# Cross attention to 257 keys: row maxima taken one head group at a time, with picks and one copy in another order

## The chip, the cores and the metric

One core of a Trainium2 chip. The metric is the device time of one execution of the whole kernel in microseconds (us); less is better. PE is TensorE's matmul, PEld its weight load, DVE VectorE, ACT ScalarE, POOL GpSimd, SP the engine that issues most DMAs.

## The reference

A four-layer perceiver-like model on x of shape (128, 32, 128), with a context of (128, 257, 128). Three of its sublayers are cross attention of 32 queries per batch to the 257 context rows, 16 heads of width 8, 128 batches each. The one with a mask (the other two are alike but for weights and biases):

```python
query = _split_heads(q @ wq.T + bq)
key_h = _split_heads(k @ wk.T + bk)
value = _split_heads(v @ wv.T + bv)
scores = jnp.einsum('bhqd,bhkd->bhqk', query, key_h) * scale
scores = jnp.where(mask == 0, jnp.float32(-1000000000.0), scores)
attn = jax.nn.softmax(scores, axis=-1)
x = jnp.einsum('bhqk,bhkd->bhqd', attn, value)
return x.transpose(0, 2, 1, 3).reshape(...) @ wo.T + bo
```

The result is added to x. The other sublayers (self attention, routed experts, a linear transformer, retention, feed-forward blocks) are not touched by the change.

## The kernel before

The function `cross_attention` runs three times, as a_cross, e_cross and t_cross; t_cross has the mask, and e_cross also collects the results of experts that ran before it (GpSimd fetches them, VectorE adds them). Each run is one block in which every engine has its own program, written out by hand as a function `step(i, n)`: i counts turns, n the N = 8 batches of a turn, and `turns` repeats it as a hardware loop over 128 batches. Order on an engine is the order of these calls; between engines only semaphores order the work.

Per batch the 16 heads form G = 4 groups of 4 heads. The scores of a group, 128 rows (4 heads x 32 queries) by 257 keys, fill one PSUM bank of their own, banks 0 to 3. The fifth bank (K_BANK) holds kT's projection of the next batch and, later in the step, the second turned half of E; the sixth (V_BANK) the projected values and, beside them, side products; the seventh (T_BANK) the first turned half; the eighth (O_BANK) the weighted values of four batches.

- TensorE, step n: scores(n) (line 2332; 2337 adds the mask), after all four exponentials of n - 1; the projection of the keys of n + 1 (line 2316), after ScalarE has copied the second half of n - 3 out of the same bank; side products; first turn of n - 2 (line 2390); values' projection of n + 1 (2320); second turn of n - 2 (2390), which waits for VectorE's copy of the projected keys, in the same bank; weighted values of n - 3 (2400).
- VectorE, step n: reciprocals of n - 1 (2530); in each fourth step (n % 4 = 3) three picks (2567), which add the right rows of O_BANK into aT, each after the one before; maxima of groups 0 and 1 in one instruction (2520); copy of the projected keys with their bias (2534); maxima of groups 2 and 3; the fourth pick; statistics in each fourth step; copy of the first turned half of n - 2 (2526); other side work (2548, 2542, 2555), which waits for ScalarE's values' copy of n + 1.
- ScalarE, step n: in each fourth step the copy that begins aT (2453); copy of the values of n (2471); copy of the second turned half of n - 3 (2467); side copies; four exponentials (2477), one per group, with the row sums. The first waits for the first pair of maxima, the third for the second pair; each reads its group's column of negtop.
- GpSimd, step n: E times the reciprocals for n - 1 (2251), and side work.

The maxima are double-buffered in negtop. The values and E have a buffer for each of eight batches.

Of the kernel before, what the change touches and what calls it, by code (L numbers as in the profile page):

```python
# [2113 lines left out]
def cross_attention(core, name, weights, context, scale, mask=None, rest=None, behind=None):  # L2114
# [10 lines left out]
    N, G, J = 8, 4, 4  # L2125
# [4 lines left out]
    with Scope(core, name) as sc:  # L2130
# [35 lines left out]
        s_score, s_top, s_exp, s_inv, s_unit = sc.sem("score"), sc.sem("top"), sc.sem("exp"), sc.sem("inv"), sc.sem("unit")  # L2166
# [16 lines left out]
        def exists(i, n):  # L2183

            return not isinstance(i, int) or 0 <= i * N + n < B

        def tile_exists(i, t):

            return not isinstance(i, int) or 0 <= i * 2 + t < TILES
# [5 lines left out]
        def turns(eng, step, written=1):  # L2195

            for i in range(written):
                for n in range(N):
                    step(i, n)
            with eng.Fori(written, TURNS - 1) as i:  # L2200
                for n in range(N):
                    step(i, n)
            for n in range(N + 7):
                step(TURNS - 1, n)
# [8 lines left out]
        @block.sync  # L2213
        def _(sp):
            fetch(sp)
            for h in range(2):
                sp.dma_start(ctx_sb[:, h], context[:, h]).then_inc(s_ctx[h], 16)
            if rest is not None:
                rest[0](sp)
            if mask is not None:  # L2220
                for j in range(4):
                    sp.dma_start(mask_int[j * S:(j + 1) * S], mask).then_inc(s_mask, 16)
            with sp.Fori(1, TURNS) as i:
                for h in range(2):
                    sp.wait_ge(s_vl, i * 2 - 1 + h)
                    sp.dma_start(ctx_sb[:, h:h + 1], context[:, bass.ds(i * 2 + h, 1)]).then_inc(s_ctx[h], 16)
# [202 lines left out]
        @block.scalar  # L2429
        def _(act):  # L2430
            arrived(act)
            act.wait_ge(s_ready, 1)

            def queries(i, t):
                act.wait_ge(s_qp, i * 2 + t + 1)
                act.activation(qT[:, t % 2], psum[:, V_BANK, SIDE], ACT.Identity, bias=bq[:], scale=scale).then_inc(s_q, 1)

            def turned(i, t):
                act.wait_ge(s_turned, i * 2 + t + 1)
                if tile_exists(i, t - 2):  # L2440
                    act.wait_ge(s_qp, i * 2 + t - 1)
                act.activation(hT[:, t % 2], psum[:, V_BANK, BESIDE], ACT.Copy).then_inc(s_hT, 1)

            def begin(i, n):

                t = n // 4
                if n % 4 == 2 and tile_exists(i, t - 1):
                    if exists(i, n + 1):
                        act.wait_ge(s_vp, i * N + n + 2)
                    act.wait_ge(s_alone, i * 2 + t)  # L2450
                    if tile_exists(i, t - 3):
                        act.wait_ge(s_out, i * 2 + t - 2)
                    act.activation(aT[:, (t - 1) % 2], psum[:, V_BANK, SIDE], ACT.Copy).then_inc(s_begun, 1)

            def side_out(i, n):

                t = n // 4
                if n % 4 == 0 and tile_exists(i, t + 1):
                    queries(i, t + 1)
                if n % 4 == 2 and tile_exists(i, t + 2):  # L2460
                    turned(i, t + 2)

            def second_half(i, n):
                act.wait_ge(s_t1, i * N + n + 1)
                if exists(i, n - 2):
                    act.wait_ge(s_pv, i * N + n - 1)
                act.activation(ET[:, n % 2, 1], psum[:, K_BANK], ACT.Copy).then_inc(s_ET1, 1)  # L2467

            def values_out(i, n):
                act.wait_ge(s_vp, i * N + n + 1)  # L2470
                act.activation(v_sb[:, n % N].rearrange("p c d -> p (c d)"), psum[:, V_BANK, 0:2 * P], ACT.Copy).then_inc(s_v, 1)

            def exponentials(i, n):
                for g in range(G):
                    if g % 2 == 0:
                        act.wait_ge(s_top, (i * N + n) * 2 + g // 2 + 1)
                    act.activation(E[:, n % N, g], psum[:, g, 0:SK], ACT.Exp, bias=negtop[:, n % 2, g:g + 1],  # L2477
                                   accum_out=total[:, n % 2, g:g + 1]).then_inc(s_exp, 1)

            def step(i, n):  # L2480
                begin(i, n - 1)
                if exists(i, n):
                    values_out(i, n)
                if exists(i, n - 3):
                    second_half(i, n - 3)
                side_out(i, n - 1)
                if exists(i, n):
                    exponentials(i, n)

            turned(0, 0)  # L2490
            queries(0, 0)
            turned(0, 1)
            turns(act, step)

        @block.vector
        def _(dve):
            def statistics(i, t):
                u, at = t % 2, i * 2 + t
                if tile_exists(i, t - 2):
                    gate(dve, s_centred, at - 1, passed)  # L2500
                dve.bn_stats(stats[:, u], x_tile(i, t)).then_inc(s_stats, 1)
                gate(dve, s_stats, at + 1, passed)
                dve.bn_aggr(moments[:, u], stats[:, u]).then_inc(s_moments, 1)
# [9 lines left out]
                dve.tensor_copy(fold_bf[:], spread(core.const("fold"), J, 1)).then_inc(s_mask_ready, 1)  # L2513
                dve.tensor_scalar(mask_neg[:], mask_int[:], 0.0, -1e30, ALU.is_equal, ALU.mult).then_inc(s_mask_ready, 1)

            def maximum(i, n, half):
                if half == 0:
                    dve.wait_ge(s_score, i * N + n + 1)
                at = slice(2 * half, 2 * half + 2)
                dve.tensor_reduce(negtop[:, n % 2, at], psum[:, at, 0:SK], AX.X, ALU.max, negate=True).then_inc(s_top, 1)  # L2520

            def first_half(i, n):
# [5 lines left out]
            def reciprocals(i, n):  # L2528
                dve.wait_ge(s_exp, (i * N + n) * G + G)
                dve.reciprocal(inverse[:, n % 4], total[:, n % 2]).then_inc(s_inv, 1)  # L2530

            def keys(i, n):
                dve.wait_ge(s_kp, i * N + n + 1)
                dve.tensor_scalar(kT[:, n % 2], psum[:, K_BANK, 0:SK], w("bk"), None, ALU.add).then_inc(s_k, 1)
# [23 lines left out]
            def pick(i, t, places):  # L2558

                out = aT[:, t % 2].rearrange("p (b s) -> p b s", s=S)  # L2560
                for j in places:
                    if j == 0:
                        dve.wait_ge(s_begun, i * 2 + t + 1)
                        dve.wait_ge(s_pv, i * N + 4 * t + 4)
                    else:
                        dve.wait_ge(s_picked, (i * 2 + t) * 3 + j)
                    dve.scalar_tensor_tensor(out=out, in0=psum[:, O_BANK].rearrange("p (b j s) -> p b j s", b=BPT, s=S)[:, :, j],
                                             scalar=in_group[:, j:j + 1], in1=out, op0=ALU.mult, op1=ALU.add
                                             ).then_inc(s_aT if j == J - 1 else s_picked, 1)
# [11 lines left out]
            def step(i, n):  # L2581
                picks = n % 4 == 3 and tile_exists(i, n // 4 - 1)
                if exists(i, n - 1):
                    reciprocals(i, n - 1)
                if picks:
                    pick(i, n // 4 - 1, (0, 1, 2))
                if exists(i, n):
                    maximum(i, n, 0)
                if exists(i, n + 1):
                    keys(i, n + 1)  # L2590
                if exists(i, n):
                    maximum(i, n, 1)
                if picks:
                    pick(i, n // 4 - 1, (3,))
                if rest is not None and isinstance(i, int) and i == 0 and n == 0:
                    rest[1](dve)
                if n % 4 == 0 and tile_exists(i, n // 4 + 2):
                    statistics(i, n // 4 + 2)
                if exists(i, n - 2):
                    first_half(i, n - 2)  # L2600
                ahead = (i, n - 3) if n >= 3 else (i - 1, n + N - 3)
                if fetch_of(*ahead) is not None:
                    add_result(fetch_of(*ahead))
                if n % 4 == 1 and tile_exists(i, n // 4 - 1):
                    last_weights(i, n // 4 - 1, n + 1)
                if n % 4 == 1 and tile_exists(i, n // 4 - 2):
                    output(i, n // 4 - 2, n + 1)
                if n % 4 == 3 and tile_exists(i, n // 4):
                    last_values(i, n // 4, n + 1)
# [914 lines left out]
```

## Time and profile before

| | |
|---|---|
| median of 3 runs | 3989.83 us (3988.98 to 3995.96) |
| the profiled execution | 3982.57 us |
| its span, first to last instruction | 3980.8 us |
| busy over the span: PE, DVE, ACT, POOL | 3385.2 (85%), 2670.8 (67%), 2362.3 (59%), 2422.3 (61%) us |
| mean granted TensorE clock | 0.925 of full speed |
| first and last scores' matmul of a_cross, e_cross, t_cross | 18.1 to 502.3, 2145.2 to 2630.0, 2887.7 to 3373.1 us |

The three stages lie at the start, in the middle and late in the span; together they are some 1455 of 3981 us. A share over the whole span says little of them. A step of n can be told in the timeline by its scores' matmul, and n % 4 by the side work: the picks stand in n % 4 = 3, the statistics in n % 4 = 0. I call the steps with n % 4 = 0, 1, 2, 3 A, B, C and D.

### The profile page before, as it was taken

The page shows a single profiled execution, that of the slowest core. Times are in us where ns is not written, and L with a number is a line of the kernel's source. Part 1 is how long each engine was busy: PE and PEld are TensorE (multiplying, and loading weights), DVE is VectorE, ACT ScalarE, POOL GpSimd, SP SyncE. Part 2 cuts the span into 40 slices and gives each one's busy share as a digit, 9 for nine tenths or more (in the row PEclk, how much of TensorE's full clock was granted, in tenths as well). Part 3 has the DMA queues.
Part 4 walks back from the last instruction along what each step waited for, and adds up shares of the span by engine and source line. Part 5 has one row for each costly group of instructions (what it writes and reads, how often), then busy time and mean ns, then how long its engine had stood idle before and what let it go on. Part 6 is the DMA issues. An engine that isn't in the chain of part 4 may idle for free. (4 is left out here: it accounts for less than half of the span.)

```text
span 3980.8 us, 119953 instructions
## 1 busy us (share of the span) xinstructions
PE 3385.2 (85%) x44674; PEld 2469.3 (62%) x44674; DVE 2670.8 (67%) x7002; ACT 2362.3 (59%) x6308; POOL 2422.3 (61%) x2724
## 2 busy tenths in 40 slices
PE   7999959999999579698698999978499999786866
PEld 5777737777777467365466777745277777453444
DVE  6888757777777523477445888857778887754655
ACT  6777736666666334386124777745577777644633
POOL 6767656776777343574425887746367676845733
PEclk9999979999999689898799999989599999887968
DMA  2111110000000122101221111110011111000023
GB/s 75 36 42 36 36 70 6 8 11 11 8 6 2 63 72 77 47 14 47 67 72 59 51 45 42 37 60 4 17 37 36 42 36 30 3 2 6 2 93 94
DMA packets 90549, 149.05 MB, mean 37 GB/s; under 512 B 10112, under 2 KB 66816, under 8 KB 89664
## 3 DMA queue, kind: packets, MB, share of 16 engines
q1 hardware_dynamic: 79936, 122.87, 9.9%
q0 software_dynamic: 10240, 20.99, 1.7%
q8 instruction: 261, 4.28, 0.4%
q14 instruction: 112, 0.92, 0.1%
HBM read 112.76 MB, written 31.06 MB: 36 GB/s over the span
## 5 line engine op out<-in xcount | busy, mean ns | idle before, releaser
L2251 POOL TENSOR_TENSOR t_cross_E<-t_cross_E,t_cross_inverse 128x1028 f32<-128x1028 f32 x128 | 243.2, 1900 | 134.8 <-DVE t_cross_inverse L2530 134.8
L2251 POOL TENSOR_TENSOR a_cross_E<-a_cross_E,a_cross_inverse 128x1028 f32<-128x1028 f32 x128 | 243.2, 1900 | 132.8 <-DVE a_cross_inverse L2530 132.8
L2477 ACT ACTIVATE t_cross_E<-t_cross_psum,t_cross_negtop 128x257 f32<-128x257 f32 x512 | 238.8, 472 | 113.5 <-DVE t_cross_negtop L2520 110.0
L2477 ACT ACTIVATE a_cross_E<-a_cross_psum,a_cross_negtop 128x257 f32<-128x257 f32 x512 | 238.8, 472 | 112.4 <-DVE a_cross_negtop L2520 103.9
L2477 ACT ACTIVATE e_cross_E<-e_cross_psum,e_cross_negtop 128x257 f32<-128x257 f32 x512 | 238.8, 472 | 111.2 <-DVE e_cross_negtop L2520 103.3
L2251 POOL TENSOR_TENSOR e_cross_E<-e_cross_E,e_cross_inverse 128x1028 f32<-128x1028 f32 x128 | 243.2, 1900 | 94.2 <-DVE e_cross_inverse L2530 94.1
L3090 PEld LDWEIGHTS l_psum<-l_ffn_w,l_hidden 128*128 128x128 f32 x1536 | 197.9, 192 | 98.0 <-issue 56.1
L3090 PE MATMUL l_psum<-l_ffn_w,l_hidden 128*128 128x128 f32 x1536 | 207.8, 278 | 19.0 <-POOL l_hidden L2963 17.9
L3083 PE MATMUL l_psum<-l_hT,l_ffn_w 128*128 128x512 f32 x384 | 200.6, 625 | 0.9 <-ACT l_hT L3139 0.9
L2520 DVE TENSOR_REDUCE t_cross_negtop<-t_cross_psum 128x2 f32<-128x514 f32 x256 | 175.8, 687 | 32.6 <-PE t_cross_psum L2337 31.7
L2520 DVE TENSOR_REDUCE a_cross_negtop<-a_cross_psum 128x2 f32<-128x514 f32 x256 | 175.4, 686 | 26.8 <-PE a_cross_psum L2332 26.4
L2520 DVE TENSOR_REDUCE e_cross_negtop<-e_cross_psum 128x2 f32<-128x514 f32 x256 | 175.6, 686 | 24.6 <-PE e_cross_psum L2332 24.5
L2942 POOL TENSOR_SCALAR l_normed<-inner,l_moments,l_rstd 128x128 f32<-128x128 f32 x192 | 149.8, 793 | 14.8 <-POOL l_rstd L2936 14.8
L2390 PE MATMUL e_cross_psum<-const_sb,e_cross_E 128*128 128x128 f32 x1024 | 154.3, 274 | 0.2
L2390 PE MATMUL a_cross_psum<-const_sb,a_cross_E 128*128 128x128 f32 x1024 | 153.4, 273 | 0.2
L2390 PE MATMUL t_cross_psum<-const_sb,t_cross_E 128*128 128x128 f32 x1024 | 153.4, 273 | 0.2
L2953 POOL TENSOR_TENSOR l_q<-l_q,l_q_stat 128x512 f32<-128x512 f32 x48 | 50.8, 1058 | 167.3 <-DVE l_q_stat L3217 167.3
L2963 POOL TENSOR_TENSOR l_hidden<-l_hidden,l_less 128x512 f32<-128x512 f32 x96 | 122.2, 1293 | 18.2 <-ACT l_hidden L3163 18.2
L1467 POOL DMA_INDIRECT slots<-hT_all,behind_place_i x64 | 61.7, 965 | 111.5 <-PE c_moe_psum L1600 61.9
L1467 POOL DMA_INDIRECT slots<-inner,a_moe_place_i x64 | 62.0, 969 | 101.6 <-PE a_moe_psum L1600 59.0
L3237 DVE TENSOR_TENSOR inner<-l_psum,inner 128x512 f32<-128x512 f32 x48 | 33.2, 692 | 132.1 <-PE l_psum L3075 132.1
L2390 PEld LDWEIGHTS e_cross_psum<-const_sb,e_cross_E 128*128 128x128 f32 x1024 | 121.2, 142 | 0.9 <-ACT e_cross_ET L2467 0.4
(754 smaller groups left out, 11124.1 us busy)
## 6 DMA issues: line engine op xcount, KB each, us to landing
a_cross_context<-context SPq DMA_DIRECT2D x32, 578.0 KB, 3.7
e_cross_context<-context SPq DMA_DIRECT2D x32, 578.0 KB, 3.7
t_cross_context<-context SPq DMA_DIRECT2D x32, 578.0 KB, 3.7
u_moe_weights<-pack_u_moe SPq DMA_DIRECT2D x1, 5633.0 KB, 16.3
slots<-l_blank SPq DMA_DIRECT2D x6, 832.0 KB, 12.2
a_moe_x_slots<-slots SPq DMA_DIRECT2D x26, 192.0 KB, 2.8
slots<-a_moe_y_slots SPq DMA_DIRECT2D x26, 192.0 KB, 2.1
c_moe_x_slots<-slots SPq DMA_DIRECT2D x26, 192.0 KB, 2.8
```

What stands on the lines that cost most here:

```text
L1467: pool.indirect_dma_start(slots.halves[g], bass.IndirectOffsetOnAxis(ap=place_i[:, k, at:at + 1], axis=0), rows[:, at], None).then_inc(s_p ...
L2251: pool.tensor_tensor(E[:, n % N], E[:, n % N], spread(inverse[:, n % 4], SK, 2), ALU.mult).then_inc(s_unit, 1)
L2390: last = pe.transpose(psum[:, (T_BANK, K_BANK)[c], g * P:(g + 1) * P], E[:, n % N, g, c * P:(c + 1) * P], ident)
L2477: act.activation(E[:, n % N, g], psum[:, g, 0:SK], ACT.Exp, bias=negtop[:, n % 2, g:g + 1], accum_out=total[:, n % 2, g:g + 1]).then_inc(s ...
L2520: dve.tensor_reduce(negtop[:, n % 2, at], psum[:, at, 0:SK], AX.X, ALU.max, negate=True).then_inc(s_top, 1)
L2942: last = pool.tensor_scalar(Y1[:, t], c.tile(t), moments[:, 0, t, 0:1], rstd[:, 0, 1, t:t + 1], ALU.subtract, ALU.mult)
L2953: pool.tensor_tensor(groups, groups, spread(q_stat[:, 2], DH, 2), ALU.mult).then_inc(s_soft, 1)
L2963: pool.tensor_tensor(hidden[:, f], hidden[:, f], less[:, f - 2], ALU.add).then_inc(s_late, 1)
L3083: pe.matmul(psum[:, U_BANKS[f % 2]], c.ffn(f * P), hT2[:], start=True, stop=True).then_inc(s_up, 1)
L3090: last = pe.matmul(psum[:, D_BANK, t * P:(t + 1) * P], hidden[:, f, t * P:(t + 1) * P], c.ffn((NF + f) * P), start=(f == 0 and t == 0), st ...
L3237: dve.tensor_tensor(c.chunk(), tiles(psum[:, C_BANK]), c.chunk(), ALU.add).then_inc(s_mid, 1)
```

## The change

The maxima are taken for one group at a time: four instructions of 128x257 in place of two of 128x514. Three of them now stand ahead of the keys' copy and one behind. The semaphore s_top counts four per batch, and each of ScalarE's exponentials waits for its own group's maximum. The picks of n % 4 = 3 were 0, 1, 2 ahead of the first maxima and 3 behind the last; now pick 0 is ahead of the maxima, pick 1 between the second and third maximum, picks 2 and 3 behind the fourth. On ScalarE the copy of the second turned half goes ahead of the values' copy where n is odd; where it is even the values stay first. Nothing else is changed; the arithmetic is the same.

```diff
@@ scalar: exponentials, step
                 for g in range(G):
-                    if g % 2 == 0:
-                        act.wait_ge(s_top, (i * N + n) * 2 + g // 2 + 1)
+                    act.wait_ge(s_top, (i * N + n) * G + g + 1)
                     act.activation(E[:, n % N, g], psum[:, g, 0:SK], ACT.Exp, bias=negtop[:, n % 2, g:g + 1],
...
                 begin(i, n - 1)
-                if exists(i, n):
+                if exists(i, n) and n % 2 == 0:
                     values_out(i, n)
                 if exists(i, n - 3):
                     second_half(i, n - 3)
+                if exists(i, n) and n % 2 == 1:
+                    values_out(i, n)
                 side_out(i, n - 1)
@@ vector: maximum, step
-            def maximum(i, n, half):
-                if half == 0:
+            def maximum(i, n, g):
+                if g == 0:
                     dve.wait_ge(s_score, i * N + n + 1)
-                at = slice(2 * half, 2 * half + 2)
+                at = slice(g, g + 1)
                 dve.tensor_reduce(negtop[:, n % 2, at], psum[:, at, 0:SK], AX.X, ALU.max, negate=True).then_inc(s_top, 1)
...
                 if picks:
-                    pick(i, n // 4 - 1, (0, 1, 2))
+                    pick(i, n // 4 - 1, (0,))
                 if exists(i, n):
                     maximum(i, n, 0)
+                    maximum(i, n, 1)
+                if picks:
+                    pick(i, n // 4 - 1, (1,))
+                if exists(i, n):
+                    maximum(i, n, 2)
                 if exists(i, n + 1):
                     keys(i, n + 1)
                 if exists(i, n):
-                    maximum(i, n, 1)
+                    maximum(i, n, 3)
                 if picks:
-                    pick(i, n // 4 - 1, (3,))
+                    pick(i, n // 4 - 1, (2, 3))
```

## Rows read from the trace of the kernel before

**Rows 1.** Windows view, first attention stage: us of window, busy per engine, clock, DMA.

```profile
16.00:506.00 490.00, 457.52 (x5145) 347.90 (x5145) 389.22 (x915) 375.70 (x1371) 339.03 (x342) 1.00 0.13 39
```

**Rows 2.** View of line 2520: who waited for it, us, times.

```profile
  ACT a_cross_E L2477: 103.9, 143
```

**Rows 3.** View of line 2332: ns min/median/max, first and last start.

```profile
L2332 PE MATMUL a_cross_psum<-a_cross_kT,a_cross_q_heads x1024: 375/450/792, 18.1 to 502.3; 32*128 32x257 f32 x171
...
L2332 PE MATMUL t_cross_psum<-t_cross_kT,t_cross_q_heads x1024: 375/450/792, 2887.7 to 3373.1; 32*128 32x257 f32 x171
```

**Rows 4.** Timeline, step A: start, length, engine, line, names, [idle before].

```profile
307.92 0.71 PE L2332 MATMUL a_cross_psum<-a_cross_kT,a_cross_q_heads 32*128 32x257 f32 x8
...
308.70 0.69 DVE L2520 TENSOR_REDUCE a_cross_negtop<-a_cross_psum 128x2 f32<-128x514 f32 x1 [0.15 <-PE a_cross_psum L2332]
...
308.77 0.67 PE L2316 MATMUL a_cross_psum<-a_cross_context,a_cross_weights 128*128 128x257 f32 x2
...
309.43 0.48 ACT L2477 ACTIVATE a_cross_E<-a_cross_psum,a_cross_negtop 128x257 f32<-128x257 f32 x1 [0.80 <-DVE a_cross_negtop L2520]
309.49 0.49 DVE L2534 TENSOR_SCALAR a_cross_kT<-a_cross_psum,a_cross_weights 128x257 f32<-128x257 f32 x1
...
309.89 0.68 DVE L2520 TENSOR_REDUCE a_cross_negtop<-a_cross_psum 128x2 f32<-128x514 f32 x1
...
310.39 0.60 PE L2390 MATMUL a_cross_psum<-const_sb,a_cross_E 128*128 128x128 f32 x4
...
310.61 0.48 ACT L2477 ACTIVATE a_cross_E<-a_cross_psum,a_cross_negtop 128x257 f32<-128x257 f32 x1
...
310.92 0.38 PEld L2400 LDWEIGHTS a_cross_psum<-a_cross_ET,a_cross_v 128*32 128x32 f32 x16 [0.17 <-issue]
...
311.07 0.47 ACT L2477 ACTIVATE a_cross_E<-a_cross_psum,a_cross_negtop 128x257 f32<-128x257 f32 x1
...
311.52 0.38 ACT L2471 ACTIVATE a_cross_v<-a_cross_psum 128x256 f32<-128x256 f32 x1
...
311.68 0.72 PE L2332 MATMUL a_cross_psum<-a_cross_kT,a_cross_q_heads 32*128 32x257 f32 x8
...
311.79 0.60 ACT L2467 ACTIVATE a_cross_ET<-a_cross_psum 128x512 f32<-128x512 f32 x1
```

**Rows 5.** Timeline, step D, the one ahead of it.

```profile
303.95 0.72 PE L2332 MATMUL a_cross_psum<-a_cross_kT,a_cross_q_heads 32*128 32x257 f32 x8
304.10 1.12 DVE L2567 SCALAR_TENSOR_TENSOR a_cross_aT<-a_cross_psum,const_sb,a_cross_aT 128x128 f32<-128x128 f32 x3
...
305.14 0.68 DVE L2520 TENSOR_REDUCE a_cross_negtop<-a_cross_psum 128x2 f32<-128x514 f32 x1
...
306.58 0.60 PE L2390 MATMUL a_cross_psum<-const_sb,a_cross_E 128*128 128x128 f32 x4
...
307.18 0.41 PEld L2400 LDWEIGHTS a_cross_psum<-a_cross_ET,a_cross_v 128*32 128x32 f32 x16 [0.24 <-issue]
```

**Rows 6.** Groups by form, VectorE maximum of 128 columns.

```profile
L1321 DVE TENSOR_REDUCE c_moe_best<-c_moe_cand 128x16 f32<-128x128 f32 x4 | 1.1, 286 | 0.1
```

**Rows 7.** Timeline, projection and second turn, steps C and B.

```profile
301.04 0.67 PE L2316 MATMUL a_cross_psum<-a_cross_context,a_cross_weights 128*128 128x257 f32 x2
...
302.76 0.60 PE L2390 MATMUL a_cross_psum<-const_sb,a_cross_E 128*128 128x128 f32 x4
...
312.54 0.67 PE L2316 MATMUL a_cross_psum<-a_cross_context,a_cross_weights 128*128 128x257 f32 x2
...
314.37 0.60 PE L2390 MATMUL a_cross_psum<-const_sb,a_cross_E 128*128 128x128 f32 x4
```

**Rows 8.** Timeline, stage with the mask: scores and first maxima.

```profile
3102.32 0.72 PE L2332 MATMUL t_cross_psum<-t_cross_kT,t_cross_q_heads 32*128 32x257 f32 x8
...
3103.18 0.69 DVE L2520 TENSOR_REDUCE t_cross_negtop<-t_cross_psum 128x2 f32<-128x514 f32 x1
```

**Rows 9.** Timeline, GpSimd, the stage that collects expert results.

```profile
2299.26 1.90 POOL L2251 TENSOR_TENSOR e_cross_E<-e_cross_E,e_cross_inverse 128x1028 f32<-128x1028 f32 x1 [1.41 <-DVE e_cross_inverse L2530]
```

## The prediction

> **What bounds the kernel now.** I first took the busy time of the engines over one of the three attention stages to 257 keys [rows 1]. No engine is full: TensorE shows 457.5 of 490 us, VectorE 389.2, ScalarE 375.7, GpSimd 339.0, at a granted clock of 1.00 (the 2.4 GHz level). Each engine waits for another one once per batch. The list of who waited for line 2520 then names the largest wait in the stage: ScalarE's exponentials wait 103.9 us for the negated maxima, in 143 places [rows 2]. The scores' matmuls show the length of a batch: from 18.1 to 502.3 us for 128 batches, less the 0.5 us that lie inside one batch, over 127 intervals, is 3.81 us; the stage with the mask takes the same (2887.7 to 3373.1) [rows 3]. Four batches, over which the side work repeats, take 15.24 us.
>
> Then the timeline of one step, n % 4 = 0, step A [rows 4]; times from here on are counted from the start of the scores' matmul, S (307.92). First pair of maxima +0.78, first exponential +1.51, kT projection +0.85, its copy by VectorE ("keys") +1.57, second pair +1.97, third exponential +2.69, fourth +3.15, next scores +3.76. The chain that sets the length: the copy of values and then of the second turned half (0.27 apart, 0.60 long) free the bank that kT's projection writes; the projection gives the keys' copy; behind that stands the second pair of maxima, and behind that the third exponential, which starts 0.04 after the pair ends (309.89 + 0.68 = 310.57, 310.61). Counted from e, the start of the fourth exponential: values +0.45, second half +0.72, its end +1.32, projection +1.46, keys' copy +0.72 later, second pair +0.40, third exponential +0.72, fourth +0.47: e to e is 3.77. That is steps A, B and C. In step D (n % 4 = 3) three picks of 1.12 us precede the first pair, which starts at +1.19 and not +0.78, and aT's copy delays the rest: 307.92 - 303.95 = 3.97 [rows 5]. Three times 3.77 and 3.97 are 15.28, against 15.24 measured, so I trust this chain.
>
> **The change part by part.** (1) *Four maxima of 257 in place of two of 514.* No row shows a 128x257 maximum. The pair of 514 takes 0.68 us [rows 4] and one of 128 columns 0.286 [rows 6]; the line between them gives 0.42 for 257. A VectorE instruction that waits for nothing starts 0.08 before the end of the one ahead (keys 309.49 with 0.49, then 309.89) [rows 4]. So a maximum takes 0.34 of the queue and a pair 0.68 - 0.08 = 0.60: the split costs 2 x (2 x 0.34 - 0.60) = 0.16 us of VectorE per batch. The gain: the first exponential waits for 0.42 and not 0.68, so it starts at +1.24 (+1.51 now). The bounds of the spacing are 0.34 and 0.42 (the full duration); I take 0.34, since the keys' copy has the same width and shows the overlap.
>
> (2) *Three maxima ahead of the keys' copy.* The third exponential no longer hangs on the projection. The maxima start at +0.78, 1.12, 1.46, the keys' copy at +1.80 to 2.28, the fourth maximum +2.20 to 2.62. Exponentials every 0.47: +1.24, 1.71, 2.18, 2.65; the fourth needs 2.62 + 0.04, so none waits again. Next scores by this route: 2.65 + 0.61 (311.07 to 311.68) = 3.26. The added waits of ScalarE for the second and fourth maximum are therefore met; queued behind them are only the exponentials and copies of the same step.
>
> But the keys' copy is now later after S, and the second turn on TensorE (it writes the bank that the copy reads) waits for it. Today the copy ends at +2.06 and that turn starts at +2.47, no stall. Afterwards it can start at +2.34 (2.28 + 0.06, the smallest wake-up in these steps, an estimate). From that turn to the end of the values' weight loads are 0.91 us (310.39 to 310.92 + 0.38) [rows 4], then the scores may load. In front of those loads stand the three waits of the scores; the weighted values, also behind waits long met, show 0.17 to 0.24 idle "issue" [rows 4, 5], so the gap is between 0 and 0.24 and I take 0.12. Route over TensorE: 2.34 + 0.91 + 0.12 = 3.37. This is what is late next, and step A becomes 3.37 us. The projection is not late for it: the scores now start later after e (3.73 - 2.91 = 0.82 at D to A), so it comes at 1.46 - 0.82 = +0.64.
>
> (3) *Second half ahead of the values in odd steps.* The bank is free at e + 1.05, so the projection comes 0.27 earlier. The values' copy comes at e + 0.93 and ends +1.31, before the side product that needs it; the next values' projection is later still. VectorE's three waits for a values' copy (last weights, output, last values) all name an even batch, whose order stays. In step B, whose turn comes 1.83 after the projection [rows 7], 0.55 + 1.83 = 2.38 against 2.34 from the keys: 3.41. Without this part the projection would be at +0.77 and the step 3.63: it is worth 0.2 us in two of four steps at most, since in D the keys decide anyway. Step C, with values first: projection 1.46 - 0.76 = +0.70, its turn 1.72 later [rows 7], 2.42: 3.45.
>
> (4) *Picks.* In D the first pick alone (about 0.35, after aT's copy) ends before the scores are there, so the first maximum is back at +0.78: a gain of 0.41. The second pick adds 0.26 to the queue (0.34 less the overlap) ahead of the keys: their copy ends at 2.54, the turn starts at 2.60, from there 1.01 (306.58 to 307.18 + 0.41) [rows 5] and 0.12: 3.73. The fourth exponential starts at 2.84 + 0.08 = about 2.91, next scores 3.52 by that route; TensorE decides. Picks three and four and the copy of the first half move behind the fourth maximum and end near +4.25, beyond the next scores by 0.5; the reader of that half comes 1.4 after those scores, and the next maximum waits for scores until +0.78: hidden, with about 0.1 to spare. If that cover is gone each 0.1 costs 32 x 0.1 = 3 us per stage.
>
> (5) *Sum.* 3.37 + 3.41 + 3.45 + 3.73 = 13.96 for four, 1.28 less, 32 times: 41 us per stage. With the mask the scores are ready 0.08 later (+0.86 for +0.78) [rows 8]; today the projection hides that, afterwards it is on the path in all four steps: 14.28, gain 31. In the stage that also collects expert results GpSimd idles 1.41 us per four batches in its first half [rows 9], so its floor is 15.24 - 1.41 = 13.83, just under 13.96; I take 39. Together 111 us. The profiled execution is 3982.57 us (span 3980.8), 7.3 below the median of 3989.83; 3982.6 - 111 = 3871.6, and on the median 3878.8.
>
> The page "VectorE: DVE Perf Modes" of the Trainium skill, section "The DRAIN you can't avoid", speaks against this change: it says that the next operation does not start until the pipe has emptied, and advises fewer operations. The trace does not show it so strictly (the 0.08 us overlap above); by the rule the spacing would be the full 0.42 us, which is the first rival below.
>
> **The rivals.** *Spacing equal to the duration* (0.42 between maxima, 0.34 behind a pick): keys end at 2.52, turn 2.58, step 3.61 three times; D has keys to 2.86, turn 2.92, step 4.05. Sum 14.88, gain 11.5 us in two stages and none with the mask: 3967 us. Against it: the keys' copy and the pair behind it overlap [rows 4].
>
> *TensorE's busy time is a floor.* 457.5 of 490 us [rows 1] leaves 32.5 per stage, 97.5 in all: 3892 us. Against it: busy times overlap; the second turn's 0.60 us end at 310.99, behind the next loads' start at 310.92 [rows 4]. The skill's page "Trainium Kernel Development and Optimization", section "Performance Expectations", calls matmul busy time a bad metric for this reason.
>
> *Slower: a single maximum costs nearly what a pair costs.* Place: VectorE's queue between the scores and the keys' copy, with the second turn behind it. Each us of spacing over 0.34 counts three times per step: 13.96 + 12 x (s - 0.34) = 15.24 gives s = 0.45 as the point from which the change loses. At the pair's 0.60 the four steps take 17.1, 1.85 more, 32 x 3 times: 4167 us. Against it: the 128-column maximum at 0.286 shows that width is paid for. For it: the margin is only 0.11 us, and the width of 257 was not measured.
>
> *It does nothing that counts*: an unseen wait (a context load, GpSimd) holds the step at 15.2: 3990 us. The waits of before show none.
>
> **How the numbers follow.** Forecast 0.72 (3836 to 3920); spacing 0.08; TensorE's floor 0.09; slower 0.06; nothing 0.05. The low end is the gap at zero in front of the scores (13.48 per four, 56 + 56 + 46 us gained: 3832), which I cut slightly; the high end goes halfway to the first rival (0.38 of spacing: 13.96 + 0.48, about 3925) and a little over, 3935. Left outside are the rivals at 3967, 3990 and 4167, 0.19. A difference of 0.2% (8 us) is about what can be told from none: faster 0.90, within 0.04, slower 0.06.
>
> **What would show it.** Right: 128x257 maxima of 0.42 us at 0.34 spacing; no wait of the exponentials for the maxima after the first; scores that start behind the values' loads and not behind the exponentials; VectorE's idle nearly gone; 13.9 to 14.0 us per four batches, a bit more with the mask. Wrong: maxima of over 0.5 us, a second turn later than +2.6 in steps A to C, a first maximum later than +0.8 in A (tail of D uncovered), GpSimd without idle time in the collecting stage, or a granted clock under 1.00 there.

## The result and the profile after

| | before | after |
|---|---|---|
| median | 3989.4 us (4 runs) | 3963.6 us (3962.2 to 3967.4, 4 runs) |
| ratio | | 0.993, 95% interval 0.9915 to 0.9945 |
| span of the profiled execution | 3980.8 us | 3960.4 us |
| four batches, a_cross, e_cross, t_cross | 15.23, 15.25, 15.27 us | 14.85, 14.83, 15.23 us |

The change brings 26 us where 111 were forecast; the time lies outside the range of the prediction, and the direction is right. The last row of the table is worked out as in the prediction, from the first and the last scores' matmul (less 0.5 us, over 127 intervals, times 4). Its savings of 0.38, 0.42 and 0.04 us, 32 times each, are 27 us, which is all of the difference; the stage with the mask gained next to nothing. The ratio is taken from the runs; the stages are read from one profiled execution of each kernel.

The view of the scores' line after the change, answering to [rows 3]: line, engine, count, length in ns (min/median/max), first and last start in us.

```profile
L2332 PE MATMUL a_cross_psum<-a_cross_kT,a_cross_q_heads x1024: 375/474/792, 18.1 to 490.2; 32*128 32x257 f32 x171
...
L2332 PE MATMUL e_cross_psum<-e_cross_kT,e_cross_q_heads x1024: 375/474/792, 2135.8 to 2607.2; 32*128 32x257 f32 x171
...
L2332 PE MATMUL t_cross_psum<-t_cross_kT,t_cross_q_heads x1024: 375/474/792, 2866.5 to 3350.5; 32*128 32x257 f32 x171
```

The maxima, now at line 2521, and who waited for them, answering to [rows 2]:

```profile
L2521 DVE TENSOR_REDUCE a_cross_negtop<-a_cross_psum x512: 411/415/427, 19.4 to 491.9; 128x1 f32<-128x257 f32 x171
...
  ACT a_cross_E L2476: 107.5, 158
```

The windows view of the first stage, answering to [rows 1]:

```profile
16.00:506.00 490.00, 461.59 (x5213) 353.01 (x5213) 401.50 (x1196) 369.53 (x1374) 344.44 (x347) 1.00 0.14 41
```

A single maximum takes 0.415 us, as interpolated, and the granted clock is 1.00 as before. But ScalarE waits for the maxima as long as before, 107.5 us against 103.9: the wait was not removed, it moved. Ahead of the first exponential of step A it is 1.25 us now and was 0.80 in [rows 4]. VectorE is 401.5 us busy of 490, not nearly full, though the forecast expected that.

Step A, answering to [rows 4]. Here x3 is three instructions merged into one row.

```profile
300.52 0.31 PEld L2332 LDWEIGHTS a_cross_psum<-a_cross_kT,a_cross_q_heads 32*128 32x128 f32 x8 [0.20 <-issue]
300.52 0.71 PE L2332 MATMUL a_cross_psum<-a_cross_kT,a_cross_q_heads 32*128 32x257 f32 x8
...
301.17 0.30 PEld L2316 LDWEIGHTS a_cross_psum<-a_cross_context,a_cross_weights 128*128 128x128 f32 x2 [0.33 <-issue]
301.17 0.70 PE L2316 MATMUL a_cross_psum<-a_cross_context,a_cross_weights 128*128 128x257 f32 x2
301.30 1.09 DVE L2521 TENSOR_REDUCE a_cross_negtop<-a_cross_psum 128x1 f32<-128x257 f32 x3 [0.63 <-PE a_cross_psum L2332]
...
301.76 0.48 ACT L2476 ACTIVATE a_cross_E<-a_cross_psum,a_cross_negtop 128x257 f32<-128x257 f32 x1 [1.25 <-DVE a_cross_negtop L2521]
...
302.31 0.48 DVE L2535 TENSOR_SCALAR a_cross_kT<-a_cross_psum,a_cross_weights 128x257 f32<-128x257 f32 x1
...
302.84 0.66 PE L2390 MATMUL a_cross_psum<-const_sb,a_cross_E 128*128 128x128 f32 x4
...
303.15 0.47 ACT L2476 ACTIVATE a_cross_E<-a_cross_psum,a_cross_negtop 128x257 f32<-128x257 f32 x1
303.43 0.38 PEld L2400 LDWEIGHTS a_cross_psum<-a_cross_ET,a_cross_v 128*32 128x32 f32 x16 [0.17 <-issue]
...
304.00 0.72 PE L2332 MATMUL a_cross_psum<-a_cross_kT,a_cross_q_heads 32*128 32x257 f32 x8
```

Counted from the scores (300.52): projection +0.65, maxima +0.78, first exponential +1.24, keys' copy +1.79, second turn +2.32, fourth exponential +2.63, weighted values' loads +2.91, next scores +3.48. The prediction had +0.64, 0.78, 1.24, 1.80, 2.34, 2.65, 2.87 and 3.37. Up to the second turn it holds within 0.02 us.

Step D, answering to [rows 5]:

```profile
311.12 0.72 PE L2332 MATMUL a_cross_psum<-a_cross_kT,a_cross_q_heads 32*128 32x257 f32 x8
311.33 0.35 DVE L2568 SCALAR_TENSOR_TENSOR a_cross_aT<-a_cross_psum,const_sb,a_cross_aT 128x128 f32<-128x128 f32 x1 [0.30 <-PE a_cross_psum L2400]
...
311.90 0.76 DVE L2521 TENSOR_REDUCE a_cross_negtop<-a_cross_psum 128x1 f32<-128x257 f32 x2 [0.23 <-PE a_cross_psum L2332]
...
312.58 0.34 DVE L2568 SCALAR_TENSOR_TENSOR a_cross_aT<-a_cross_psum,const_sb,a_cross_aT 128x128 f32<-128x128 f32 x1
...
313.17 0.48 DVE L2535 TENSOR_SCALAR a_cross_kT<-a_cross_psum,a_cross_weights 128x257 f32<-128x257 f32 x1
...
313.70 0.66 PE L2390 MATMUL a_cross_psum<-const_sb,a_cross_E 128*128 128x128 f32 x4
313.89 0.73 DVE L2568 SCALAR_TENSOR_TENSOR a_cross_aT<-a_cross_psum,const_sb,a_cross_aT 128x128 f32<-128x128 f32 x2
314.01 0.47 ACT L2476 ACTIVATE a_cross_E<-a_cross_psum,a_cross_negtop 128x257 f32<-128x257 f32 x1 [0.16 <-DVE a_cross_negtop L2521]
...
314.73 0.41 PEld L2400 LDWEIGHTS a_cross_psum<-a_cross_ET,a_cross_v 128*32 128x32 f32 x16 [0.61 <-issue]
...
314.76 0.64 PE L2400 MATMUL a_cross_psum<-a_cross_ET,a_cross_v 128*32 128x128 f32 x16 [0.41 <-DVE a_cross_aT L2568]
...
315.52 0.32 PEld L2332 LDWEIGHTS a_cross_psum<-a_cross_kT,a_cross_q_heads 32*128 32x128 f32 x8 [0.38 <-issue]
315.52 0.72 PE L2332 MATMUL a_cross_psum<-a_cross_kT,a_cross_q_heads 32*128 32x257 f32 x8
```

Counted from 311.12: first pick +0.21, maxima +0.78 and +1.12, second pick +1.46, keys' copy +2.05, second turn +2.58, picks three and four +2.77 to 3.50, fourth exponential +2.89. All of this is where it was forecast. Then the weights of the weighted values are loaded at +3.61 and not at +3.20 (2.60 + 0.60, as the prediction's 3.73 implies), and D takes 4.40 us; this is a D with n = 7, the last step of a hardware-loop turn; with n = 3 it takes 4.22. The row says why: TensorE sat idle 0.41 us until VectorE's write of aT, that is until pick 4. The weighted values of step D are those of batch n - 3, the first of the next four. They write the bank that the picks read (O_BANK), so the code of `values` makes them wait for the last pick (semaphore s_aT) where n - 3 is a multiple of 4. The fourth pick used to stand directly behind the maxima:

```profile
306.73 0.34 DVE L2567 SCALAR_TENSOR_TENSOR a_cross_aT<-a_cross_psum,const_sb,a_cross_aT 128x128 f32<-128x128 f32 x1
```

It ended at 307.07 and the weighted values' loads of [rows 5] began 0.11 us later, with 0.24 us of idle time called "issue" where step A showed 0.17. So this wait already ended last in the kernel before and put the loads off by some 0.07 us; the next scores waited for the exponentials there. TensorE's idle time ahead of line 2400 in the changed kernel, by what ended it (us, times). The first row is of all three stages and steps, the second of the first stage, 31 of its 32 steps D:

```profile
  issue: 108.1, 381
...
  DVE a_cross_aT L2568: 13.5, 31
```

The steps of the changed kernel in the first stage are A 3.48, B 3.62, C 3.50, D 4.22 and 4.40 in turn. They were forecast as 3.37, 3.41, 3.45 and 3.73.

### The profile page after: what moved, and what is told of

It reads as the page before. It is cut to its first block and busy times, and to the rows that moved or that the text cites. A ratio compares the mean times of both kernels' runs of the same rounds, so it can differ in the third digit from the quotient of the medians.

```text
span 3960.4 us, 121393 instructions
## 1 busy us (share of the span) xinstructions
PE 3382.5 (85%) x44674; PEld 2471.5 (62%) x44674; DVE 2693.2 (68%) x7770; ACT 2337.6 (59%) x6308; POOL 2421.8 (61%) x2724
## 5 line engine op out<-in xcount | busy, mean ns | idle before, releaser
L2476 ACT ACTIVATE a_cross_E<-a_cross_psum,a_cross_negtop 128x257 f32<-128x257 f32 x512 | 238.5, 473 | 107.6 <-DVE a_cross_negtop L2521 107.5
L2521 DVE TENSOR_REDUCE t_cross_negtop<-t_cross_psum 128x1 f32<-128x257 f32 x512 | 194.9, 417 | 65.3 <-PE t_cross_psum L2337 65.3
L2521 DVE TENSOR_REDUCE a_cross_negtop<-a_cross_psum 128x1 f32<-128x257 f32 x512 | 194.9, 417 | 53.4 <-PE a_cross_psum L2332 53.4
L2521 DVE TENSOR_REDUCE e_cross_negtop<-e_cross_psum 128x1 f32<-128x257 f32 x512 | 195.0, 417 | 47.9 <-PE e_cross_psum L2332 44.6
L2390 PEld LDWEIGHTS a_cross_psum<-const_sb,a_cross_E 128*128 128x128 f32 x1024 | 116.1, 141 | 12.6 <-DVE a_cross_kT L2535 10.0
```

What stands on the lines that cost most here:

```text
L2390: last = pe.transpose(psum[:, (T_BANK, K_BANK)[c], g * P:(g + 1) * P], E[:, n % N, g, c * P:(c + 1) * P], ident)
```

## The experiments

T1 is the theory that in step D the weighted values wait for pick 4; T2, that VectorE's queue as a whole is full around D, whatever its order; T3, that in the other steps TensorE's own queue decides. Picks are counted from 1 in the text and from 0 in the code and in some expectations: pick 4 is `pick(..., (3,))`. The ratios are to the kernel before, on the same chip.

The picks stand at another place in most of these kernels. Step D with n = 3 in the first stage, us from the start of its scores:

| kernel | last pick ends | weighted values' loads start | next scores |
|---|---|---|---|
| before | 3.12 | 3.24 | 3.97 |
| changed | 3.50 | 3.62 | 4.22 |
| the picks put back | 3.31 | 3.43 | 4.03 |
| two picks one operation later | 4.10 | 4.21 | 4.82 |
| the split alone | 3.31 | 3.43 | 4.03 |
| step D interleaved | 2.84 | 2.96 | 3.83 |

The loads start 0.11 or 0.12 us behind the end of the last pick in every kernel. In the four in the middle the next scores follow them by 0.60 or 0.61 us; in the first and the last the fourth exponential ends later and decides.

### The picks put back

```diff
-                    pick(i, n // 4 - 1, (0,))
+                    pick(i, n // 4 - 1, (0, 1, 2))
...
-                if picks:
-                    pick(i, n // 4 - 1, (1,))
...
-                    pick(i, n // 4 - 1, (2, 3))
+                    pick(i, n // 4 - 1, (3,))
```

> The changed kernel with only its picks put back (picks 0 to 2 ahead of the maxima, pick 3 behind the fourth maximum). Theory T1 (in step D the weighted values of the next four batches write the bank that the picks read, and wait for pick 3): pick 3 ends about 0.3 us earlier in D than in the changed kernel, though three picks stand ahead of the first maximum again; D about 4.05 instead of 4.25 us on the mean, 3946 us in all (3935 to 3955), under the changed kernel's 3963.6. Theory T2 (VectorE's queue as a whole is full around D and its tail delays what follows): the same work in another order, 3963. The forecast on record, by which the new place of the picks is worth 0.41 us per D: slower than the changed kernel, about 3995.

Measured: 3946.3 us, ratio 0.9894 (0.9874 to 0.9913). T1 gave 3946. The same work on VectorE in the old order is 17 us faster, against T2; and against the forecast, by which the old order had to be slower (about 3995). Step D starts its first maximum at +1.25 again and its second turn at +2.78, both later than in the changed kernel, but the last pick is at +2.97 (one of 0.34) where the changed kernel has a pair from +2.77 to +3.50. The weighted values start at +3.45, and D takes 4.03 and 4.24 us:

```profile
293.05 0.72 PE L2332 MATMUL a_cross_psum<-a_cross_kT,a_cross_q_heads 32*128 32x257 f32 x8
...
296.02 0.34 DVE L2568 SCALAR_TENSOR_TENSOR a_cross_aT<-a_cross_psum,const_sb,a_cross_aT 128x128 f32<-128x128 f32 x1
...
296.48 0.41 PEld L2400 LDWEIGHTS a_cross_psum<-a_cross_ET,a_cross_v 128*32 128x32 f32 x16 [0.23 <-issue]
```

The last pick still ends last here, but only just: behind the second turn alone the loads could start at +3.37 (2.78 + the 0.59 of step A above, an estimate), and they start at +3.43. The idle time ahead of line 2400 is back to what it was in the kernel before (72.4 us of "issue"):

```profile
  issue: 72.5, 381
  DVE a_cross_aT L2568: 1.0, 1
```

### Two picks one operation later

```diff
-                if picks:
-                    pick(i, n // 4 - 1, (2, 3))
...
                 if exists(i, n - 2):
                     first_half(i, n - 2)
+                if picks:
+                    pick(i, n // 4 - 1, (2, 3))
```

> The changed kernel with picks 2 and 3 moved one more operation back, behind the copy of the first turned half (0.68 us). T1: pick 3 and with it the weighted values come 0.6 us later in every D, 96 times: 3963.6 + 58 = about 4021 us. T2 (total of VectorE's queue): unchanged, 3963. The forecast on record (picks 2 and 3 are hidden there): unchanged or a few us faster, as the first half comes earlier.

Measured: 4018.2 us, ratio 1.0064 (1.0049 to 1.0079). T1 gave 4021; T2 and the forecast gave no change. Two picks moved by one place cost 55 us and make the kernel slower than the one before. Its step D:

```profile
307.09 0.72 PE L2332 MATMUL a_cross_psum<-a_cross_kT,a_cross_q_heads 32*128 32x257 f32 x8
...
309.86 0.68 DVE L2527 COPY a_cross_ET<-a_cross_psum 128x512 f32<-128x512 f32 x1
...
310.46 0.73 DVE L2568 SCALAR_TENSOR_TENSOR a_cross_aT<-a_cross_psum,const_sb,a_cross_aT 128x128 f32<-128x128 f32 x2
...
311.33 0.65 PE L2400 MATMUL a_cross_psum<-a_cross_ET,a_cross_v 128*32 128x128 f32 x16 [1.01 <-ACT a_cross_ET L2467]
...
311.91 0.72 PE L2332 MATMUL a_cross_psum<-a_cross_kT,a_cross_q_heads 32*128 32x257 f32 x8
```

The pair of picks starts 0.60 us behind the start of the copy of the first half (0.68 long) and ends at 311.19, +4.10; the weighted values follow at +4.24, the next scores at +4.82. The profile names a copy by ScalarE as the releaser. By the code that is not what they wait for: they need both turned halves of batch n - 3, which were copied in step n - 1 and early in step n, and the last pick. The copy by ScalarE that ends at 311.31 is that of the next batch, and the weights are loaded from 311.30 on, before its end and 0.11 us behind that of the pick.

### Step D interleaved

```diff
 # the new order in step D alone; the other steps keep that of the changed kernel
+                    pick(i, n // 4 - 1, (0, 1))
                     maximum(i, n, 0)
                     maximum(i, n, 1)
+                    keys(i, n + 1)
+                    pick(i, n // 4 - 1, (2,))
                     maximum(i, n, 2)
+                    pick(i, n // 4 - 1, (3,))
                     maximum(i, n, 3)
```

> The changed kernel with another order in step D alone: picks 0, 1, maxima 0, 1, the keys' copy, pick 2, maximum 2, pick 3, maximum 3. T1: pick 3 ends near +2.9 instead of +3.5 and more, the fourth exponential starts near +3.2; D falls from 4.25 to about 3.9 us, 96 x 0.35 = 34 us: 3930 us (3920 to 3940), faster than both kernels. T2: 3963. A theory in which the exponentials alone set D: maxima 2 and 3 are later than in the changed kernel by 0.2 and 0.3 us, so slower by up to 25 us: 3989.

Measured: 3927.0 us, ratio 0.9837 (0.9822 to 0.9852), where T1 gave 3930. This is the fastest kernel of the study by median, some 65 us (0.0163 x 3990) under the one before and 37 under the changed one. Its step D:

```profile
304.02 0.72 PE L2332 MATMUL a_cross_psum<-a_cross_kT,a_cross_q_heads 32*128 32x257 f32 x8
...
306.52 0.34 DVE L2568 SCALAR_TENSOR_TENSOR a_cross_aT<-a_cross_psum,const_sb,a_cross_aT 128x128 f32<-128x128 f32 x1
306.64 0.47 ACT L2476 ACTIVATE a_cross_E<-a_cross_psum,a_cross_negtop 128x257 f32<-128x257 f32 x1 [0.29 <-DVE a_cross_negtop L2521]
...
307.01 0.64 PE L2400 MATMUL a_cross_psum<-a_cross_ET,a_cross_v 128*32 128x128 f32 x16
...
307.85 0.72 PE L2332 MATMUL a_cross_psum<-a_cross_kT,a_cross_q_heads 32*128 32x257 f32 x8 [0.19 <-ACT a_cross_E L2476]
```

Pick 4 starts at +2.50, the weighted values at +2.99, and D takes 3.83 us with n = 3 and with n = 7 alike. Now the exponentials decide: TensorE's wait for the scores names ScalarE. Maxima 2 and 3 are later here than in the changed kernel by 0.45 and 0.33 us (+2.17 and +2.76), and the step is shorter all the same, so the exponentials alone had not set D. The next step pays a little: A is 3.57, since ScalarE's second half comes later after these late exponentials, and the projection starts at +0.76 or +0.85.

### Values first in every step

```diff
-                if exists(i, n) and n % 2 == 0:
+                if exists(i, n):
                     values_out(i, n)
                 if exists(i, n - 3):
                     second_half(i, n - 3)
-                if exists(i, n) and n % 2 == 1:
-                    values_out(i, n)
```

> The changed kernel with the values' copy ahead of the second turned half in all steps, as before. The forecast on record: step B loses 0.2 us, D nothing, 32 x 3 times: +19 us, 3983. T3 (after the split, TensorE's own queue decides when the projection of the keys starts, +0.65 in every step whatever ScalarE's order): 3962 to 3967, no difference.

Measured: 3969.3 us, ratio 0.9942 (0.9929 to 0.9956), inside the changed kernel's interval. The forecast gave 3983. The stages themselves do not differ at all:

```profile
L2332 PE MATMUL a_cross_psum<-a_cross_kT,a_cross_q_heads x1024: 375/474/792, 18.0 to 490.2; 32*128 32x257 f32 x171
...
L2332 PE MATMUL t_cross_psum<-t_cross_kT,t_cross_q_heads x1024: 375/474/792, 2877.6 to 3361.9; 32*128 32x257 f32 x171
```

That is 14.86 and 15.24 us for four batches, against 14.85 and 15.23. In step B the projection starts at +0.65 with either order; in D it moves from +0.64 to +0.77, and nobody waits for it there. The 7 us between the two profiled spans lie outside the three stages, where the programs are alike: the stretch between the first two stages takes 1652.0 us here and 1645.6 in the changed kernel, and between the last two 263.8 at a granted clock of 0.71 against 259.3 at 0.75. So ScalarE's new order is worth nothing in the changed kernel. That it may be worth something elsewhere is argued at the kernel with the split alone, below.

### Less work on TensorE, after and before

```diff
-                for c in range(2):
+                for c in range(1):
                     last = pe.matmul(psum[:, V_BANK, c * P:(c + 1) * P], keys_of(n)[:, c * P:(c + 1) * P], w("wv"),
...
-                act.activation(v_sb[:, n % N].rearrange("p c d -> p (c d)"), psum[:, V_BANK, 0:2 * P], ACT.Copy)
+                act.activation(v_sb[:, n % N], psum[:, V_BANK, 0:P].unsqueeze(1).to_broadcast([P, 2, P]), ACT.Copy)
```

> The changed kernel with less work on TensorE: only the first half of the values is projected (two of the four matmuls of that line, about 0.22 us of TensorE's queue per batch), and ScalarE's copy of the same size reads that half twice; the second half of the values is left out of the computation, all other instructions and waits stay. T3 (after the split TensorE's own queue sets steps A, B and C, and the picks set D): A to C lose up to 0.22 us each until the exponentials' route of 3.26 us decides, D nothing: 3963.6 - 3 x 32 x 3 x 0.2 = about 3906 us (3895 to 3920). A theory in which the exponentials or VectorE's queue set A to C: unchanged, 3960 or more.

Measured: 3964.7 us, ratio 0.9928 (0.9912 to 0.9945). T3 as I had put it fails. Four batches take 14.71, 14.72 and 15.08 us, 0.14 less than in the changed kernel and not 0.6; those 13 us do not show in the total, because the part between a_cross and e_cross takes longer here, 1659.1 us against 1645.6. In the eight kernels that compute the same result it takes 1642.9 to 1652.0. The values that this part gets are not the same here, and the experts' work may depend on them; that was not tried. So this kernel is to be read by its stages. One of its steps B:

```profile
301.20 0.72 PE L2332 MATMUL a_cross_psum<-a_cross_kT,a_cross_q_heads 32*128 32x257 f32 x8
...
302.99 0.48 DVE L2535 TENSOR_SCALAR a_cross_kT<-a_cross_psum,a_cross_weights 128x257 f32<-128x257 f32 x1
...
303.53 0.66 PE L2390 MATMUL a_cross_psum<-const_sb,a_cross_E 128*128 128x128 f32 x4
...
304.11 0.64 PE L2400 MATMUL a_cross_psum<-a_cross_ET,a_cross_v 128*32 128x128 f32 x16
...
304.69 0.72 PE L2332 MATMUL a_cross_psum<-a_cross_kT,a_cross_q_heads 32*128 32x257 f32 x8
```

The keys' copy ends at +2.27 and the second turn starts at +2.33. In the changed kernel it starts at +2.51 in B, +2.39 in C and +2.32 in A; with 0.22 us less work ahead of it, it starts at +2.32 or +2.33 in all three, and A, B and C all take 3.48 or 3.49 us. A, which has lost the same work, is as long as before. What TensorE waits for ahead of its turns, in the first stage (us, times), in this kernel:

```profile
  DVE a_cross_kT L2535: 42.9, 127
```

and in the changed kernel, where the 32 are the steps D:

```profile
  DVE a_cross_kT L2535: 10.0, 32
```

This is the bound that the prediction named, the turn behind the keys' copy, at the very time that it gave (+2.34). In the whole changed kernel it decides A; in B, where two side products stand ahead, and in C TensorE's own queue decides.

> The kernel before with the same cut (second half of the values left out, 0.22 us less on TensorE per batch). By the chain of the prediction (ScalarE's second half, the keys' projection, the keys' copy, the second pair of maxima, the third exponential), which passes over TensorE only ahead of the values' projection: no change, 3980 to 3990 us. If TensorE's queue already was the bound of the kernel before: as much as in the changed kernel, about 3935.

Measured: 4006.0 us, ratio 1.0028 (1.0017 to 1.004). The stages are again unmoved: four batches take 15.26 us.

```profile
L2332 PE MATMUL a_cross_psum<-a_cross_kT,a_cross_q_heads x1024: 375/450/792, 17.9 to 503.0; 32*128 32x257 f32 x171
```

The extra time lies between the stages, as above: e_cross starts at 2157.9 us, 12.7 later than before, behind an a_cross that is less than 1 us longer. TensorE's queue was not the bound of the kernel before, and its 457 of 490 us of busy time were no floor.

### The split alone

```diff
 # the kernel before, with s_top counted by group and
                     maximum(i, n, 0)
+                    maximum(i, n, 1)
                     keys(i, n + 1)
-                    maximum(i, n, 1)
+                    maximum(i, n, 2)
+                    maximum(i, n, 3)
```

> The kernel before with only the maxima split: groups 0 and 1 ahead of the keys' copy, 2 and 3 behind it, each exponential behind its own maximum; picks and ScalarE's order as before. By the chain: the third exponential waits for 0.42 and not 0.68 us behind the keys' copy, so steps A to C fall from 3.77 to about 3.5 us (there TensorE's queue stands too), D from 3.97 to about 3.8: 14.35 for four, 3990 - 96 x 0.88 = about 3905 us, faster than the changed kernel. If the place of the keys' copy (third maximum ahead of it) is what brought the changed kernel's gain: no faster than 3963.

Measured: 3953.2 us, ratio 0.9894 (0.9877 to 0.991). Faster than the changed kernel, so the place of the keys' copy is not what brought the gain, but far from the 3905 that the chain gave. Step A takes 3.40 us, where 3.5 was expected. B takes 3.77: its projection starts at +0.83, since A is short and ScalarE still copies the values first. Here the other order should pay: the changed kernel's B takes 3.62. No kernel with this one difference was run. And D takes 4.03 and 4.22, with the fourth pick at +2.97 and the weighted values at +3.46: the same gate. Four batches take 14.77, 14.82 and 14.96 us.

### The keys' copy third in every step

```diff
 # the interleaved kernel (e4), with keys(i, n + 1) behind maximum(i, n, 1) for all n
```

> The interleaved order of e4 with the keys' copy behind the second maximum in every step, not only in D. T3: the second turn no longer waits 0.04 us for the keys' copy in A and up to 0.1 with the mask: 0 to 10 us under e4's 3927. If the third exponential falls behind the later maxima instead: slower than e4 by 96 x 0.1 = 10 us.

Measured: 3932.7 us, ratio 0.9854 (0.9837 to 0.987); the intervals of this kernel and of the interleaved one overlap. Four batches take 14.48, 14.56 and 14.73 us, against 14.49, 14.54 and 14.75: no difference. The earlier copy helps only where the second turn had waited for it: every other A takes 3.51 and not 3.57 us, some 1 us per stage. In the other A, in B and in C the turn starts where it did (+2.46, +2.51, +2.40). The third and fourth exponentials come 0.14 to 0.25 us later, and the next scores do not.

## Why the prediction was wrong

- **The chain of the kernel before** held. It gave the steps of before to 0.05 us, but for the two around the end of a loop turn (4.05 and 3.64 where n = 7 and n = 0), and with less work on TensorE the stage stayed as long.
- **Part 1, the split**: held. 0.415 us long and 0.34 apart (three in 1.09 us, which is 0.415 + 2 x 0.34). The rule of the Trainium skill that I set against it ("VectorE: DVE Perf Modes", "The DRAIN you can't avoid") would have these three take 1.25 us, and the trace does not agree. The prediction left out the end of that paragraph of the section: that a next operation that is not held starts earlier. With that the trace agrees, and it puts the overlap at 0.08 us. The advice for fewer operations stands in another section of the same page of the Trainium skill, "Rules for kernel authors".
- **Part 2, the second turn is late next**: the mechanism and its time held (+2.34 forecast, +2.32 measured, shown by the shortened kernel). The tail behind it was mis-sized: 0.59 us to the weighted values' loads and 0.57 on to the scores, 1.16 in all and not 1.03. I had taken 0.53 from a step in which TensorE did not wait ahead of the turn (such steps still show it: +2.51 to +3.04 in B), and 0.12 for the gap ahead of the scores, which is 0.20. That is 0.11 us in A.
- **Part 3, ScalarE's order**: wrong. It was to save 0.2 us in B and saves nothing. The projection starts at +0.64 or later in every step read; I had +0.55 for B, from no row (my own terms give 1.46 - 0.27 - 0.72 = +0.47). That is 0.10; another 0.03 lie between projection and turn and 0.08 in the tail, which makes 3.62 and not 3.41, with either order.
- **Part 4, the picks**: the step that failed. The prediction put the wait of the weighted values for the last pick at nothing. I asked who waits for the copy of the first half behind the moved picks, and not who waits for the picks. Of a moved instruction every reader and every later writer of what it reads has to be found. The wait stands in `values`, and the trace of before showed it ending last, 0.11 us behind pick 4. Forecast 3.73, measured 4.22 and 4.40: some 0.58 of the 0.89 us that four batches miss. Of the 0.58 the wait is about 0.45: without it the loads would start at +3.17 (2.58 + 0.59, an estimate) and not at +3.62. Another 0.09 on the mean is the longer end of a loop turn, and the rest the tail as in part 2. Two picks moved one place later added 0.6 us per D; moved earlier, in the interleaved kernel, they took 0.4 to 0.6 off.
- **The stage with the mask**: forecast 14.28, measured 15.23. The mask's matmuls are on the path in all steps, as forecast, with 0.08 us in A and D and 0.11 in B and C, where the projection starts at +0.75 and not at +0.65. A, B and C are 3.56, 3.73 and 3.61 us. Here too the steps' tails and D (4.30 and 4.50) take the rest.
- **The stage that collects expert results**: 14.83, as the first stage. The floor of 13.83 that I gave for GpSimd was never reached, so no run here tests it.
- **The range** covered wrong sizes of what I had seen and no wait that I had not. The rival with the full 0.42 us gave 3967, close to the result by chance: its cause is excluded by the rows.

By parts, for four batches of the first stage: the split alone takes 15.23 to 14.77. The keys' copy behind three maxima and the odd steps' order, with the picks left alone, take it to 14.67: A goes from 3.40 to 3.48, B from 3.77 to 3.61, C and D stay. (The totals of these two kernels, 3953.2 and 3946.3, have overlapping intervals, and with the mask four batches take 14.96 and 14.97.) The picks as changed bring it back to 14.85. With D interleaved, which also moves the keys' copy of that step, it is 14.49.

## What to carry to other kernels

When an instruction is moved back on its engine, list who waits for it through every buffer that it reads as well as every one that it writes: the next writer of a PSUM bank may be another engine's work for later batches, in the same step. An idle gap called "issue" that is longer in one step than in its fellows can be a wait that ended just then (0.24 us against 0.17 here), and is worth a look at the code's waits. And of the maxima, split for the sake of an early start, only the first two had to be early in this kernel: the free places between the others served best for the picks, which ended last.

## What the runs showed of the hardware that was not expected

- TensorE's weight loads stand idle 0.17 us ahead of the weighted values and 0.20 us ahead of the scores even where what they wait for has long been there ([rows 4] and the rows of step A above); between the loads of the scores and those of the keys' projection lie 0.33 us, and the projection starts at +0.64 or later in every step read. No order of the other engines that was tried made these gaps shorter.
- From the end of the last pick on VectorE to the weight load on TensorE that waits for it are 0.11 or 0.12 us, in every step D read of all kernels.
- The step that ends a turn of the hardware loop (n = 7) is 0.18 us or more longer than the other D (4.40 to 4.57 against 4.22 in the changed kernel). The time lies ahead of the scores' loads, 0.38 us idle there and not 0.20. It does not show in the interleaved kernel, where the exponentials end the step and both take 3.83; and in the kernel before the step behind it was shorter by about as much (4.05 and 3.64 against 3.97 and 3.76). Its cause was not looked for.
